# Second attention: value product last in a slot, no filler matmuls; first attention: features through DRAM and single-pass scores for chunks 1 to 3

## The reference

```python
x = x + linear_attention(layernorm(x))     # 16 heads of 8, causal; phi = elu + 1
x = x + moe(layernorm(x))                  # 16 experts, 4 per token by group routing, 2 shared
x = x + softmax_attention(layernorm(x))    # 16 heads of 8, not causal
x = x + moe(layernorm(x))                  # same weights as the first one
```

## Time and profile before

| | us |
|---|---|
| median of 3 runs (587.8 to 588.56) | 588.38 |
| the profiled execution's own time | 589.38 |
| its span, first to last instruction | 587.6 |
| first attention, first products to first expert matmul | 16.83 to 121.76 |
| second attention, first scores to next expert matmul | 284.85 to 422.96 |

### The profile page before, as it was taken

The page is one execution under the profiler, slowest core; times in us unless marked ns, Lnnn a source line. Parts: engine busy times, 40 slices in busy tenths (PEclk is TensorE's granted clock), DMA queues, the critical chain, the costliest instruction groups (busy, mean ns, idle before and its releaser), DMA issues.

```text
span 587.6 us, 12001 instructions
## 1 busy us (share of the span) xinstructions
PE 542.6 (92%) x4021; PEld 408.3 (69%) x4021; DVE 434.7 (74%) x1067; ACT 339.4 (58%) x575; POOL 317.7 (54%) x315
## 2 busy tenths in 40 slices
PE   4779897879999999999899999999999999999996
PEld 3556665657888888888555565555577888888884
DVE  3765769858889798668687787888478797886563
ACT  2473475356565655655556758676756655555553
POOL 4795887546665766777520304020155666666664
PEclk9997998999999999999879999999999999999999
DMA  6111200233354424234722433320132344344240
GB/s 171 32 43 41 75 10 1 74 76 108 107 102 125 125 90 126 90 122 162 228 95 73 149 104 117 102 71 2 45 98 87 121 125 126 96 145 128 90 149 24
DMA packets 42503, 56.62 MB, mean 96 GB/s; under 512 B 5953, under 2 KB 18258, under 8 KB 42450
## 3 DMA queue, kind: packets, MB, share of 16 engines
q1 hardware_dynamic: 39344, 55.46, 31.6%
q10 hardware_dynamic: 3106, 0.48, 0.5%
HBM read 47.27 MB, written 8.65 MB: 95 GB/s over the span
## 4 chain that ended last, share of the span: by engine, by line
PE 74%; DVE 7%; ACT 7%; POOL 4%; issue 4%; DMA 2%; SPq 1%; POOLq 0%; DVEq 0%; ACTq 0%
PE bank L814 16%; PE bank L816 16%; PE bank L815 16%; PE bank L978 6%; PE bank L923 4%; ACT PT L713 4%; DVE PT L1395 3%; PE bank L902 3%; PE bank L955 2%; PE bank L1015 2%; PE bank L938 2%; PE bank L1046 1%; ACT XN L771 1%; DVE MEXP L1415 1%; PE bank L1021 1%
## 5 line engine op out<-in xcount | busy, mean ns | idle before, releaser
L608 POOL TENSOR_TENSOR KS<-PT,QS 128x512 fp32r<-128x512 f32 x144 | 186.2, 1294 | 117.3 <-ACT QS L796 105.3
L791 ACT ACTIVATE bank<-bank 128x512 f32<-128x512 f32 x128 | 74.5, 582 | 98.8 <-PE bank L816 98.2
L1517 DVE TENSOR_TENSOR PT<-CS,bank 128x512 f32<-128x512 f32 x128 | 87.4, 683 | 45.2 <-PE bank L816 44.4
L814 PE MATMUL bank<-XH,WH 128*128 128x512 f32 (+1 forms) x288 | 114.9, 399 | 2.6 <-DVE PT L1395 1.4
L816 PE MATMUL bank<-XH,WL 128*128 128x512 f32 (+1 forms) x288 | 112.4, 390 | 0.0
L815 PE MATMUL bank<-XL,WH 128*128 128x512 f32 (+1 forms) x288 | 112.2, 389 | 0.0
L796 ACT ACTIVATE QS<-PT 128x512 fp32r<-128x512 f32 x144 | 90.1, 626 | 12.3 <-DVE PT L1522 11.8
L1415 DVE TENSOR_REDUCE MEXP<-bank 128x4 f32<-128x1024 f32 x64 | 78.1, 1223 | 25.4 <-PE bank L923 24.4
L1522 DVE TENSOR_TENSOR PT<-PT,bank 128x512 f32<-128x512 f32 x128 | 88.0, 687 | 9.5 <-ACT bank L791 1.6
L713 ACT ACTIVATE PT<-bank 128x1024 f32<-128x1024 f32 x64 | 65.5, 1024 | 40.1 <-PE bank L955 40.1
L978 PE MATMUL bank<-PT,V 128*32 128x256 f32 (+1 forms) x1024 | 64.2, 370 | 0.0
(11 more groups left out here) (181 smaller groups left out, 840.6 us busy)
## 6 DMA issues: line engine op xcount, KB each, us to landing
CS<-combine_rows SPq DMA_DIRECT2D x128, 256.0 KB, 3.2
head_rows<-HP SPq DMA_DIRECT2D x16, 256.0 KB, 3.2
QS<-head_rows SPq DMA_DIRECT2D x16, 256.0 KB, 2.7
KS<-head_rows SPq DMA_DIRECT2D x16, 256.0 KB, 3.0
head_rows<-PHI SPq DMA_DIRECT2D x8, 256.0 KB, 3.4
out_dram<-X SPq DMA_DIRECT2D x4, 256.0 KB, 3.6
stage<-in_L_ffn_gate_w_dram SPq DMA_DIRECT2D x5, 192.0 KB, 2.6
stage<-in_L_ffn_up_w_dram SPq DMA_DIRECT2D x5, 192.0 KB, 2.7
```

The source lines that it names most:

```text
L608: pool.tensor_tensor(GL[:, (u - 1) % 3, :], GG[:, (u - 1) % 3, :], GH[:, (u - 1) % 3, :].bitcast(f32), ALU.subtract).then_inc(F.gl, 1)
L791: act.activation(TH[:, u, :] if u < SHARED else G[u % 3][:, :], G[u % 3][:, :], ACT.Silu).then_inc(F.th, 1)
L814: pe.matmul(out, wh, vh, start=start, stop=False)
L1517: dve.tensor_tensor(ab, CS[:, e % CBUFS, :], U[u % 3][:, :], ALU.mult).then_inc(F.b, 1)
```

## The change

In the first attention, chunk 0 stays as it is. For chunks 1 to 3 `head_keys` is gone. The features are split by DVE (`high_rows`, a copy rounded to fp32r) and POOL (`first_low`), SP writes them to the same `head_rows` rows as the second attention uses and reads them back (`first_rows`), and `products` multiplies stacked 24-row fp32r operands. `features` of chunks 1, 2, 3 run on PE in slots 5 and 6, 12 and 13, 19 and 20 (was 7 and 8, 15 and 16, 23 and 24), on ACT and DVE one slot later. Weight pieces move from slots 7, 9, 15, 17, 23, 25 to 9, 11, 16, 18, 24, 26, and SP issues them between the row transfers. POOL's constant rows move from slot 27 to slot 2. In the second attention PE's order is half A, maxima, `output_turn`, side steps, projection or values projection (now g = 6), half B, `values_product`; `keep_clock` is gone; ACT's `output` comes after the probabilities of pair 0.

```diff
+        FEATURE_SLOT = {0: (0, 0)}
+        for c, n in ((1, 5), (2, 12), (3, 19)):
+            FEATURE_SLOT[n], FEATURE_SLOT[n + 1] = (0, c), (1, c)
-        PIECE_SLOTS = [7, 9, 15, 17, 23, 25]
+        PIECE_SLOTS = [9, 11, 16, 18, 24, 26]
...
# SP
+            def first_rows(c):
+                A = AT[0]
+                for w in range(2):
+                    sp.wait_ge(A.hi, 2 * (c - 1) + w + 1)
+                    write_rows(A, c, w, False)
+                    sp.wait_ge(A.lo, 2 * (c - 1) + w + 1)
+                    write_rows(A, c, w, True)
+                sp.wait_ge(A.qw, 16 * (4 + 6 * c))
+                for j in range(HG):
+                    if c > 1:
+                        sp.wait_ge(A.s1, 4 * (SLOTS * (c - 1) + 2 * j + 2))
+                    for w, t in enumerate((QS, KS)):
+                        sp.dma_start(t[:, j, :].bitcast(f32),
+                                     spread[w, c % 2, HG * j:HG * (j + 1)].rearrange("h s c t -> (h s c) t"))\
+                          .then_inc(A.qr[j], 16)
...
+            piece(0)
+            piece(1)
+            constant_rows()
+            for c in range(1, CHUNKS):
+                first_rows(c)
+                if c < CHUNKS - 1:
+                    piece(2 * c)
+                    piece(2 * c + 1)
# POOL
+            def first_low(w, c):
+                pool.wait_ge(AT[0].hi, 2 * (c - 1) + w + 1)
+                pool.tensor_tensor(PHI[:, w, :].bitcast(f32r), PHI[:, w, :], HP[:, w, :].bitcast(f32),
+                                   ALU.subtract).then_inc(AT[0].lo, 1)
...
-                    if cur and 2 <= g < 2 + HG:
-                        head_keys(g - 2)
+                    if 2 <= n < 2 + HG:
+                        head_keys(n - 2)
...
-                    if n == 27:
+                    if n == 2:
                         constant_rows()
...
+                    if n >= 6 and n - 1 in FEATURE_SLOT:
+                        first_low(*FEATURE_SLOT[n - 1])
# ACT, second attention
                     probabilities(1, n - 4)
-                    output()
                     if g - 1 in PROJECTION_SLOT and c + 1 < CHUNKS:
                         biased_rows(c + 1, PROJECTION_SLOT[g - 1], PJ)
                     probabilities(0, n - 4)
+                    output()
# PE, first attention
                 def products(i):
                     cc, j, b = item(i)
-                    k0, q0 = SEQ * b, cc * CHUNK + SEQ * b
-                    pe.wait_ge(A.kx, HG * cc + j + 1)
+                    k0, q0 = SEQ * b, SEQ * b
+                    if cc:
+                        pe.wait_ge(A.qr[j], 32 * cc)
+                        keys, queries, depth = KS, QS[:, j, :], 3 * HD
+                    else:
+                        pe.wait_ge(A.kx, j + 1)
+                        keys, queries, depth = KX, PQ[:, :], 32
...
-                        pe.matmul(S[h][:, 0:SEQ], KX[r, j, k0:k0 + P], PQ[r, q0:q0 + SEQ], start=True, stop=True)
+                        pe.matmul(S[h][:, 0:SEQ], keys[r, j, k0:k0 + P], queries[r, q0:q0 + SEQ], start=True, stop=True)
...
-                    if g == 7 and c + 1 < CHUNKS:
-                        features(0, c + 1)
-                    if g == 0 and 0 < c < CHUNKS:
-                        features(1, c)
+                    if n and n in FEATURE_SLOT:
+                        features(*FEATURE_SLOT[n])
# PE, second attention
                     maxima(n - 3)
                     output_turn()
-                    values_product(n - 5)
-                    scores(1, n - 2)
-                    scores_less_maxima(0, n - 4)
                     side_steps()
                     if g in PROJECTION_SLOT and c + 1 < CHUNKS:
                         projection(c + 1, PROJECTION_SLOT[g], PJ)
-                    elif g == 5 and c + 1 < CHUNKS:
+                    elif g == 6 and c + 1 < CHUNKS:
                         pe.wait_ge(A.px, 2 * c + 4)
                         values(1, c + 1, PJ)
-                    elif 4 <= n < ITEMS + 2:
-                        keep_clock(n, 1 if n % 2 == 0 and n >= 14 else 2)
+                    scores(1, n - 2)
+                    scores_less_maxima(0, n - 4)
+                    values_product(n - 5)
# DVE, first attention
+                def high_rows(w, c):
+                    dve.wait_ge(A.ph, 2 * c + w + 1)
+                    if w == 0 and c == 1:
+                        dve.wait_ge(A.kx, HG)
+                    dve.tensor_copy(HP[:, w, :], PHI[:, w, :]).then_inc(A.hi, 1)
```

More of the change, by code:

```diff
@@ L53, in __init__ @@
             self.kx = sem(prefix + "kx")
+            self.hi = sem(prefix + "hi")
             self.h3 = sem(prefix + "h3")
@@ L59, in __init__ @@
             self.px = sem(prefix + "px")
-            self.lo = sem(prefix + "lo")
-            self.qw = sem(prefix + "qw")
-            self.qr = [sem(f"{prefix}qr{j}") for j in range(4)]
             self.mt = sem(prefix + "mt")
@@ L251, in hybrid_block @@
         s_bc = sem("broadcasts_loaded")
-        s_raw = [sem(f"piece{p}_loaded") for p in range(PIECES)]
+        s_raw = [sem(f"pieces_loaded{p}") for p in range(2)]
         s_wh = sem("piece_high_done")
@@ L269, in hybrid_block @@
         LN = [NormSems(sem, f"ln{k}_", k != 2) for k in range(4)]
-        AT = [AttentionSems(sem, f"at{k}_", k) for k in range(2)]
+        s_rows_read = [sem(f"head_rows{j}_loaded") for j in range(4)]
+        AT = [AttentionSems(sem, f"at{k}_", k, s_rows_read) for k in range(2)]
         s_row_buffer = [sem(f"combine_row{i}_loaded") for i in range(CBUFS)]
@@ new lines, in piece, with constant_rows, write_rows @@
+                    sp.dma_start(dst[:, n:UPP, 2, :], sh_down.rearrange("(a f) d -> f a d", a=2)).then_inc(s_raw[p % 2], 16)
+            def constant_rows():
+                sp.wait_ge(s_cr, 1)
+                for r in range(2):
+                    for w, t in enumerate((QS, KS)):
+                        sp.dma_start(spread[w, r, :, 3, :, :], t[:, 0, :].bitcast(f32)).then_inc(AT[0].qw, 16)
+            def write_rows(A, c, w, low):
+                for part in (2 - w,) if low else (0, 1 + w):
+                    sp.dma_start(spread[w, c % 2, :, part, :, :], PHI[:, w, :] if low else HP[:, w, :].bitcast(f32))\
+                      .then_inc(A.qw, 16)
@@ L734, in slot @@
                     output()
-                    if n < ITEMS and g < 2:
-                        features(g)
+                    if n < 2:
+                        features(n, 0)
+                    elif n - 1 in FEATURE_SLOT:
+                        features(*FEATURE_SLOT[n - 1])
                     if n == 1:
@@ L1481, in slot @@
                     normalised()
-                    if n < ITEMS and g < 2:
-                        features(g)
+                    if n < 2:
+                        features(n, 0)
+                    elif n - 1 in FEATURE_SLOT:
+                        features(*FEATURE_SLOT[n - 1])
+                        high_rows(*FEATURE_SLOT[n - 1])
                     side_steps()
```

81 lines of the change are left out of this document (35 added, 46 removed).

## The result

The changed kernel takes 585.61 us in the median of 20 runs, the kernel before 587.97: a ratio of 0.9946, 95% interval 0.9925 to 0.9967. That is about 3 us gained (2.4 by the medians, 3.2 by the ratio) where 9 were forecast; 585.6 lies in the range, and faster was the likeliest sign. The profiled execution took 585.89 us. Executions of one kernel differ by several microseconds here, so verdicts go by medians and ratios, and a profile, one execution, only shows where time lies. A ratio leaves out runs over 1.5% above a kernel's fastest, so it can differ from the ratio of the medians.

A forecast was written before the change was run, and what follows sets the result against it. It saw a PE-DVE product loop plus POOL's queue bounding the first attention, and a scores-maxima-probabilities loop the second. Gains of 2.5 + 6.5 + 1 = 10 us and none in the second gave 579 us, range 571 to 590.

The forecast's parts named there:

- the likeliest sign: Whole kernel: faster at 0.81, same at 0.03, slower at 0.16, with 1.2 us as the bound for telling a change.
- Up to chunk 1: First attention's start: features and row transfers finish earlier, so chunk 1's first products come at 42.2 against 44.77, 2.5 us gained.
- Chunks 1 and 2: First attention: a shorter product loop, capped by POOL, takes 46 us instead of 52.45; 6.5 us gained, bounds 3 and 9.
- The loop term: First attention, chunks 1 and 2: products to mask 0.6 us instead of 1.04, at most 7.0 us over 16 slots.
- Chunk 3: First attention's last chunk: DVE's 21.23 us of work stays, so 1 us gained of 24.54, bounds 0 and 3.
- Second attention: Value product behind half B shortens odd slots, but side steps, later copies and low clock offset it: nothing gained, bounds +6, -4.
- a cost of the kind named: Second attention: side steps ahead of half B exceed their room, by 0.55 us in the slot with turn and projection.
- the sum of credits and debits: Second attention: 6 us gained in slots, less 2 for side steps, 2.4 for ACT's copies, 1.5 for low clock: nothing.
- The sum: Whole kernel: 10 us gained in the first attention, none in the second; 578.4 for the median, stated as 579.
- Rival (1): Second attention: without fillers PE's clock falls, 1.3 us per slow slot, 598 with 15 such slots; chance 0.15.
- Rival (2): Chunk 1's transfers or POOL's queue come late: first attention gains 2 us, second loses 1, 587.4; chance 0.14.

## Why the prediction was half right

**Up to chunk 1** (2.5 us, first products at 42.2): they came at 43.02, after a wait of 0.88 us for `KS<-head_rows`; 1.75 gained. The trip through memory, with all ahead of it, came 0.8 us later than priced. The copy `high_rows`, costed at 0.5 us, took 0.43 in the median of six, 0.74 at the longest.

**Chunks 1 and 2** (6.5 us, bounds 3 and 9): this is the step that failed. They took 52.43 us against 52.45. The loop term was right in size (0.57 from products to mask where 0.6 was taken; the products took 0.40 us up to the next matmul where 0.33 was estimated), and chunk 1 took 20.80 us. What was missing is in chunk 2. The prediction counted POOL's passes as busy time, 2.64 us each that must fit in 12.7 us of idle time, and never asked what stands behind a pass in its slot or runs beside it on VectorE. Moved one slot on, the fourth stood ahead of `scale_and_shift`, and the fifth and sixth ran beside the routing steps, which then took 4.7 us longer. Without those four passes the kernel takes 9.0 us less and chunk 2 lasts 22.10 us. Moving just the pair at 24 and 26 to 22 and 23 brings back 5.5 by the medians, of which its profile shows 0.9 in chunk 2. Moving just the fourth brings back nothing, so its place is not shown to cost anything by itself. The bound of 3 for this step would have had to be 0.

**Chunk 3** (1 us, bounds 0 and 3): 1.9.

**First expert stage** (no term): 1.9 us lost in the profile, since the stage begins at the low clock. In all eighteen profiles it takes 162.8 to 163.5 us where it begins at full clock, and 164.6 to 165.6 where it begins at the low one.

**Second attention** (0, bounds 6 gained and 4 lost): 3.3 to 4.8 gained by the kernel with that part alone, 1.5 in the profile of the changed kernel. A to B was forecast at 1.9 in odd slots and is 1.84 in the plain one; the slot with turn and projection has 2.72 from A to B at full clock, where it had 2.35, so a cost of the kind named was there. Plain odd slots gained 0.6 where 0.5 was taken, even ones 0.1. So the sum of credits and debits, put at nothing, was 3 to 5 too low.

**The sum**: 10 us were put in the first attention and none in the second. By ratios it is 0.8 in the first (from 2.4 gained to 0.9 lost) and 4.8 in the second (2.9 to 6.5). So the sign, which was right, came from the part that was to give nothing: that was luck.

**Rival (1)**, clock without fillers, was given 0.15. The clock did leave 1.00 after 305, in three stretches, but came back each time. In the old order it holds in full (14 to 21 us lost) and worst with the product in the middle. That the place of one product decides it stood in none of my steps. **Rival (2)**, rows or POOL late at 587.4 with 0.14, is nearest to what happened in the first attention, by its second half: POOL's queue, not the transfers. It had the second attention losing 1 us, which gained.

## What to carry to other kernels

An engine's idle time doesn't say that a long operation may be moved into it: look at what is next in its queue in the new slot, and at which small operations of VectorE run beside a two-input pass of POOL, since each of those can last until the pass ends. What a matmul is worth that keeps the clock up hangs on what stands behind it: 72 us lay between a useful product that closed the slot and the same one ahead of the scores that VectorE waits for, while throwaways behind it cost 10. A stage that ends at the low clock also hands it to the next: in the profile that took back half of what the first attention had gained. And when a shorter loop yields nothing, leave one suspect's work out of the kernel before moving it about: one such run sized the loss that four placements only circled.

## What the hardware showed that was not expected

A VectorE step of 16 elements took 2.48 us beside a POOL pass of 2.67 and 0.16 at its end. PE's clock fell again and again with no idle time over 1.93 us, after stretches of 3 us in which PE was busy for 1.78. With throwaways in PE's waits of the first attention, where POOL set the pace, a low clock cost little: the one run with some 20 us more of it took about 1 us longer. It is not so everywhere. In the changed kernel's twenty runs the time follows the mean clock (581.0 us at 0.966, 588.4 at 0.946), as in the twelve with the fourth piece in slot 17, and which leads to which was not separated.
